# Turning kv by VectorE blocks and a DRAM round trip instead of TensorE, in a gated cross-attention block with routed experts

## The reference, cut to what matters

```
xn = layernorm(ctx; gamma_m, beta_m);  ln = layernorm(layernorm(x); gamma_l, beta_l)
q = ln @ Wq + bq;   kv = concat(xn, ln) @ Wkv + bkv          # per batch row: 128 keys
out = softmax(q k^T / sqrt(128)) v                            # 8 heads
x = x + tanh(g_xattn) * (out @ Wo + bo)
p = softmax(layernorm(x) @ Wr + br);  two largest of 8 experts
x = x + tanh(g_ffn) * sum_e p_e * (relu(xn @ W1_e + b1_e) @ W2_e + b2_e)
```

## Time and profile before

| what | value |
|---|---|
| time, median of 3 runs (lowest to highest) | 797.5 us (796.06 to 798.2) |
| span of the profiled execution, first to last instruction | 795.7 us; a run's time is 1.8 us longer at the median |
| PE busy | 760.7 us, 96% |
| PEld, DVE, ACT, POOL busy | 81%, 66%, 62%, 56% |
| chain that ended last | PE 77%, issue 6%, POOL 6%, DVE 5%, ACT 4% |
| granted TensorE clock, mean | 0.993 |
| DMA | 119.42 MB, mean 150 GB/s |

### The profile page before, as it was taken

One profiled execution on the slowest core, in us unless ns is written; L12 is line 12 of the kernel. 1 busy time (PEld: TensorE's weight loads), 2 busy tenths in 40 slices (PEclk: granted clock), 3 DMA queues, 4 the chain that ended last, 5 costly groups with the idle time before them and its releaser, 6 DMA issues.

```text
span 795.7 us, 17460 instructions
## 1 busy us (share of the span) xinstructions
PE 760.7 (96%) x5392; PEld 643.6 (81%) x5392; DVE 528.3 (66%) x1829; ACT 496.9 (62%) x1630; POOL 446.1 (56%) x455
## 2 busy tenths in 40 slices
PE   7999999999999999999999999999999999979788
PEld 6778777777888988778988878898877888868765
DVE  5636677685857567677658776776868567565536
ACT  3677777676766566766656667565567665554522
POOL 2233264646552544785655586665568566556664
PEclk9999999999999999999999999999999999999999
DMA  7735151542454642174754226664414555634523
GB/s 198 209 150 194 60 213 69 211 146 81 145 188 154 205 153 72 38 231 143 237 189 143 65 76 218 206 212 163 127 54 140 180 191 188 212 112 116 154 77 87
DMA packets 119791, 119.42 MB, mean 150 GB/s; under 512 B 14585, under 2 KB 94994, under 8 KB 119698
## 3 DMA queue, kind: packets, MB, share of 16 engines
q1 hardware_dynamic: 111088, 102.41, 39.1%
q0 software_dynamic: 7680, 15.74, 6.8%
q10 hardware_dynamic: 930, 0.15, 0.1%
HBM read 35.94 MB, written 41.55 MB: 97 GB/s over the span
## 4 chain that ended last, share of the span: by engine, by line
PE 77%; issue 6%; POOL 6%; DVE 5%; ACT 4%; DMA 1%; another core or an unknown queue 1%; SPq 1%; POOLq 0%; ACTq 0%; DVEq 0%
PE shared L1426 13%; PE batch L1364 11%; PE batch L1377 11%; PE hid_ps L1294 8%; PE xy_ps L1308 7%; PE batch L1372 6%; PE shared L1217 3%; PE shared L1219 3%; PE shared L1218 3%; ACT probs L746 3%; PE batch L1308 2%; POOL probs L676 2%; PE xy_ps L1271 2%; POOL yg L666 2%; PE batch L1354 2%
## 5 line engine op out<-in xcount | busy, mean ns | idle before, releaser
L676 POOL TENSOR_TENSOR probs<-probs,rsums 128x512 f32<-128x512 f32 x128 | 132.9, 1039 | 231.7 <-DVE rsums L1147 230.1
L746 ACT ACTIVATE probs<-batch,neg_max 128x128 f32<-128x128 f32 x512 | 180.5, 374 | 2.0 <-DVE neg_max L1151 2.0
L651 POOL DMA_INDIRECT sorted_x<-xn,row_of x120 | 124.4, 1036 | 33.6 <-issue 28.7
L827 ACT ACTIVATE qT<-shared,tb 128x512 f32<-128x512 f32 x128 | 87.2, 696 | 85.6 <-PE shared L1219 72.4
L1377 PE MATMUL batch<-pT_sb,kvn 128*128 128x512 f32 x256 | 133.7, 604 | 2.9 <-ACT pT_sb L754 2.9
L1364 PE MATMUL batch<-kvT,qT 128*128 128x128 f32 x1024 | 135.4, 275 | 0.8 <-ACT qT L827 0.8
L1426 PE MATMUL shared<-M,oT 128*128 128x128 f32 x1024 | 125.5, 276 | 0.3
L1364 PEld LDWEIGHTS batch<-kvT,qT 128*128 128x128 f32 x1024 | 124.4, 192 | 1.2 <-ACT qT L827 1.2
L1426 PEld LDWEIGHTS shared<-M,oT 128*128 128x128 f32 x1024 | 119.4, 192 | 1.6 <-issue 1.6
L746 ACT ACTIVATION_READ_ACCUMULATOR probs<-batch,neg_max 128x1 f32 x512 | 110.2, 215 | 0.0
L1147 DVE RECIPROCAL rsums<-sums 128x4 f32<-128x4 f32 x128 | 22.7, 178 | 130.4 <-ACT probs L746 119.9
(11 more groups left out here) (168 smaller groups left out, 1243.4 us busy)
## 6 DMA issues: line engine op xcount, KB each, us to landing
wt<-wall SPq DMA_DIRECT2D x124, 321.0 KB
sorted_x<-yg SPq DMA_DIRECT2D x36, 512.0 KB, 4.8
xt<-sorted_x SPq DMA_DIRECT2D x162, 64.0 KB
sorted_y<-y_sb SPq DMA_DIRECT2D x78, 128.0 KB
kv<-in_ctx_dram SPq DMA_DIRECT2D x16, 256.0 KB
kv<-in_x_dram SPq DMA_DIRECT2D x16, 256.0 KB
xres<-in_x_dram SPq DMA_DIRECT2D x32, 128.0 KB
out_dram<-x SPq DMA_DIRECT2D x15, 256.0 KB
```

Source lines behind the costliest of these rows:

```text
L651: nc.gpsimd.indirect_dma_start(xs[k % SETS][:, :], bass.IndirectOffsetOnAxis(ap=row_of[:, g, choice, c:c + 1], axis=0), xn[:, g % 2, c, :] ...
L676: nc.gpsimd.tensor_tensor(pv, pv, rsums[:, m % 2, :].unsqueeze(2).broadcast_to([P, 4, P]), ALU.mult).then_inc(probs_ready, 1)
L746: last = nc.scalar.activation(probs[:, m % 2, c * P:(c + 1) * P], batch_ps[m % BANKS][:, c * P:(c + 1) * P], ACT.Exp, bias=neg_max[:, m % ...
L827: nc.scalar.activation(qT[:, g % 2, :, number, :], sh[:, :].rearrange("p (b i) -> p b i", b=GB), ACT.Identity, bias=tb[:, number:number + ...
```

## The change

From the second group on, kv is no longer turned on TensorE. VectorE turns it in 32x32 blocks into `kv_blocks`, half a group (four rows) at a time, right behind the shift of that half (slots 7 and 0). SP stores the blocks to a DRAM scratch array (slots 0 and 1) and, when the store has landed, loads them back with the blocks permuted into kvT (slots 1 and 2). `kv_blocks` is one buffer, so the second half's turn waits for the landing of the first half's store. kvT is laid out by blocks of 32 keys. `split_latents` moves to slot 3 and waits for both loads; so do the first scores of a group. The queries move to slots 4 to 7, two in each, at places "c", "c", "c" and "b". The first group keeps TensorE's turn, with four copies in place of each one. kvn grows from 18 to 20 rows so that the four rows of a half are adjacent, and two small tiles (`filled`, `past`) now lie in existing ones.

```diff
-KVN = 18
+KVN = 20
 ...
-    3: [("query", 1, 0, "a"), ("query", 1, 1, "b")],
-    4: [("project", 0, 0, "a"), ("turn_x", -1, 0, "b"), ("query", 1, 2, "c")],
-    5: [("router", -1, 0, "a"), ("query", 1, 3, "b"), ("query", 1, 4, "c")],
-    6: [("project", 0, 1, "a"), ("query", 1, 5, "b")],
-    7: [("query", 1, 6, "a"), ("query", 1, 7, "b")],
+    4: [("project", 0, 0, "a"), ("turn_x", -1, 0, "b"), ("query", 1, 0, "c"), ("query", 1, 1, "c")],
+    5: [("router", -1, 0, "a"), ("query", 1, 2, "c"), ("query", 1, 3, "c")],
+    6: [("project", 0, 1, "a"), ("query", 1, 4, "c"), ("query", 1, 5, "c")],
+    7: [("query", 1, 6, "b"), ("query", 1, 7, "b")],
 ...
+ and (what != "turn_kv" or g == 0)
 ...
-        kvT = sb("kvT", [P, 2, GB, P])
+        kvT = sb("kvT", [P, 2, BLOCKS, GB, BLOCK])
+        kv_blocks = sb("kv_blocks", [P, BLOCKS, 4, BLOCK])
 ...
+            def keep_blocks(g, half):
+                sp.wait_ge(blocks_turned, 2 * (g - 1) + half + 1)
+                wait(sp, got_kvT[half], 16 * (g - 1))
+                sp.dma_start(kv_turning[half], kv_blocks[:, :, :, :].rearrange("p b i j -> p (b i j)")).then_inc(blocks_kept[half], 16)
+            def load_turned(g, half):
+                sp.wait_ge(blocks_kept[half], 16 * g)
+                wait(sp, scores_ready, GB * (g - 1))
+                sp.dma_start(kvT[:, g % 2, :, 4 * half:4 * half + 4, :].rearrange("p a i j -> p a (i j)"),
+                             kv_turning[half].rearrange("(a m) (b x) -> (m b) a x", a=BLOCKS, b=BLOCKS)).then_inc(got_kvT[half], 16)
             for n in range(FIRST, LAST + 1):
                 weights(n)
                 s = n % GB
+                for half in range(2):
+                    g = n // GB + 1
+                    if s == half and 0 < g < G:
+                        keep_blocks(g, half)
+                    if s == half + 1 and 0 < g < G:
+                        load_turned(g, half)
 ...
+            def turn_blocks(n):
+                for half in range(2):
+                    g = (n - NORMALISE[2 * half + 1]) // GB
+                    if (n - NORMALISE[2 * half + 1]) % GB == 0 and 0 < g < G:
+                        dve.wait_ge(kv_ready, 4 * g + 2 * half + 2)
+                        if 2 * g + half > 2:
+                            dve.wait_ge(blocks_kept[1 - half], 16 * (g - 1 + half))
+                        first = (GB * g + 4 * half) % KVN
+                        nc.vector.transpose(kv_blocks[:, :, :, :].rearrange("p b i j -> p i b j"),
+                                            kvn[:, first:first + 4, :].rearrange("p i (m b) -> p i b m", b=BLOCKS)).then_inc(blocks_turned, 1)
             def split_latents(n, s):
-                if s == 2 and 0 <= g < G:
+                if s == (2 if g == 0 else 3) and 0 <= g < G:
+                    for half in range(2):
+                        wait(dve, got_kvT[half], 16 * g)
 ...
                 normalise_kv(n)
+                turn_blocks(n)
 ...
             def scores(m):
+                    for half in range(2):
+                        wait(pe, got_kvT[half], 16 * g)
-                                            kvT[:, g % 2, b, :], start=True, stop=True)
+                                            kvT[:, g % 2, :, b, :], start=True, stop=True)
```

More of the change, by code:

```diff
@@ L171 @@
     2: [("project", -1, 3, "a"), ("table", -2, 0, "c")],
[5 rows of a table removed]
-}
[4 rows of a table added]
+}
+BLOCK = 32
+BLOCKS = P // BLOCK
 def plan_shared():
@@ L186, in plan_shared @@
             g = n // GB + off
-            if 0 <= g < (SORTED if what == "place" else G) and (what != "table" or g in LAST_GROUP):
+            if 0 <= g < (SORTED if what == "place" else G) and (what != "table" or g in LAST_GROUP) and (what != "turn_kv" or g == 0):
                 bank = at % 2
@@ L285, in flamingo @@
         tile_id = sb("tile_id", [P, 1])
-        filled = sb("filled", [P, E, J])
+        filled = eq[:, :, :, :].rearrange("p c e f -> p (c e f)")[:, 0:E * J].rearrange("p (e j) -> p e j", e=E)
         n_tiles = sb("n_tiles", [P, E])
@@ L295, in flamingo @@
         table = sb("table", [2, NCH, P], I32)
-        past = sb("past", [P, max(CHUNKS) * 8, E - 1])
+        past = gt[:, :, :, :].rearrange("p c e f -> p (c e f)")[:, 0:max(CHUNKS) * 8 * (E - 1)].rearrange("p (m e) -> p m e", e=E - 1)
         skip = sb("skip", [P, max(CHUNKS) * 8])
@@ L361, in flamingo @@
         xs = [nc.dram_tensor(f"sorted_x{p}", (E * ROWS, D), F32).ap() for p in range(SETS)]
+        kv_turning = [nc.dram_tensor(f"kv_turning{half}", (P, BLOCKS * 4 * BLOCK), F32).ap() for half in range(2)]
         ys = [nc.dram_tensor(f"sorted_y{p}", (max(TILES) * TILE, D), F32).ap() for p in range(SETS)]
@@ L391, in flamingo @@
         kv_ready = sem("kv_ready")
+        blocks_turned = sem("blocks_turned")
+        blocks_kept = [sem("blocks_kept0"), sem("blocks_kept1")]
+        got_kvT = [sem("got_kvT0"), sem("got_kvT1")]
         scores_ready = sem("scores_ready")
@@ L821, in read_out @@
                 if what == "turn_kv":
-                    wait(act, scores_ready, GB * (g - 1))
-                    nc.scalar.activation(kvT[:, g % 2, 4 * number:4 * number + 4, :].rearrange("p b j -> p (b j)"),
-                                         sh[:, :], ACT.Copy).then_inc(shared_out[bank], 1)
+                    for b in range(4):
+                        last = nc.scalar.activation(kvT[:, g % 2, :, 4 * number + b, :], sh[:, b * P:(b + 1) * P].rearrange("p (a j) -> p a j", a=BLOCKS),
+                                                    ACT.Copy)
+                    last.then_inc(shared_out[bank], 1)
                 elif what == "query":
@@ L918, in normalise_kv @@
                     shift_kv((n - NORMALISE[k]) // GB, k)
+            def turn_blocks(n):
[8 more added lines that the diff above has]
+                                            kvn[:, first:first + 4, :].rearrange("p i (m b) -> p i b m", b=BLOCKS)).then_inc(blocks_turned, 1)
             def split_latents(n, s):
                 g = n // GB + 1
-                if s == 2 and 0 <= g < G:
+                if s == (2 if g == 0 else 3) and 0 <= g < G:
                     wait_shared(dve, shared_out, "turn_kv", g, 1)
+                    for half in range(2):
+                        wait(dve, got_kvT[half], 16 * g)
                     wait_shared(dve, shared_full, "query", g - 1, 7)
-                    nc.vector.tensor_copy(latT_hi[:, :, :], kvT[:, g % 2, :, L:P]).then_inc(latT_done, 1)
+                    mine = kvT[:, g % 2, L // BLOCK:BLOCKS, :, :].rearrange("p a b j -> p b a j")
+                    nc.vector.tensor_copy(latT_hi[:, :, :].rearrange("p b (a j) -> p b a j", j=BLOCK), mine).then_inc(latT_done, 1)
                     dve.wait_ge(latT_done, 2 * g + 1)
-                    nc.vector.tensor_tensor(latT_lo[:, :, :], kvT[:, g % 2, :, L:P], latT_hi[:, :, :].bitcast(F32),
-                                            ALU.subtract).then_inc(latT_done, 1)
+                    nc.vector.tensor_tensor(latT_lo[:, :, :].rearrange("p b (a j) -> p b a j", j=BLOCK), mine,
+                                            latT_hi[:, :, :].rearrange("p b (a j) -> p b a j", j=BLOCK).bitcast(F32), ALU.subtract).then_inc(latT_done, 1)
             def measure_rows(n, s):
```

## The result

The kernel after takes 840.62 us (median of 4 runs, 839.67 to 842.93) where the kernel before takes 797.16 in the same comparison: ratio 1.0553, 95% interval 1.0538 to 1.0567. It is slower, as forecast, but by 43.5 us where 19.7 were forecast, and outside the range of 797 to 834. A ratio with its interval is of fast runs alone, and one of e14's twelve runs, at 4334.61 us, is left out of it.

A forecast was written before the change was run, and what follows sets the result against it. Prediction: TensorE bounds slots with expert tiles, ScalarE's 3.7 us ring several slots without. Terms -5.3 - 4.2 - 3.2 - 4.0 + 9.7 + 0.7 + 19.2 + 4.8 + 2.0 = +19.7 gave 817 us, range 797 to 834.

The forecast's parts named there:

- Store, load and waits: Term for kv's round trip through DRAM and SP's queue: taken as 0, up to +20 us over 15 groups.
- the cover: Time to spare before transfers delay anyone: 0.7 us for the second half's turn, 1.5 us for its store and load.
- two copies issued in 1.14 us fit, barely: Slot 50's weight fetch on SP's queue would wait for the turn until about 253.4; its tile starts near 258.
- or SP is held by its store of the tile before: Part of the rival that kvT lands late, VectorE standing in slot 3: 837 to 847 us, chance 12%.
- I take 0.70: Time of one VectorE block turn, from the median 0.67 us of its 128x512 float32 rows; bounds 0.42 and 1.50.
- if the block turns take over 1 us: One of the signs that would show the prediction wrong: VectorE's block turns taking over 1 us.
- its own rule: VectorE's turns delay slots 0 and 1 without tiles: two turns less 0.32 and 0.13 us of gaps; term +4.8 us.
- TensorE's turn -5.3: Turn_kv leaving TensorE saves 0.88 us in each of six slots 1 with a tile, 0 in the nine without.
- The places: Queries moved: slot 3 gives -4.2, -3.2, -4.0; slots 4 to 6 with tiles +9.7, +0.7; groups without tiles +19.2 us.
- the ring of 3.7: ScalarE's chain from pT_sb through product, oT and exponentials to the next pT_sb, 3.7 us per slot whatever PE does.
- The +2.4 in slots 4 to 7: Loss per group without tiles from query work and late place "c" readouts holding ScalarE; 2.4 x 8 = +19.2 us.
- The prologue's +2.0: Start of the kernel: 8 small copies for 2, queries no longer filling gaps, first group's wait; +2.0 us, range 0 to 3.

The follow-up runs named there:

- e14: Kernel before with only groups 7, 10 and 13 turned by VectorE, their queries in the new slots, round trip right behind the fetch; ratio 0.9996.
- e1: Kernel before with only the queries' new slots and places, kv still turned on TensorE; 816.38 us.
- e3: Kernel after with the round trip moved behind the weight fetch, the tile's store and its row load on SP's queue; 833.23 us.
- e10: Kernel after with SP's order changed to weight fetch, then round trip, then the tile's store and rows; 834.73 us.
- e11: Kernel after with stores and loads cut to 16 of 128 partitions from group 2 on, the load no longer permuting; 836.08 us.
- e13: Kernel after with the changes of e10 and e11 together; 829.01 us.
- e8: Kernel before with only groups 7, 8, 10, 11, 13, 14 turned by VectorE, round trip last in SP's order, queries as before; ratio 1.0314.
- e5: Kernel before with TensorE's turn of kv and its copies left out from the third group on, nothing in their place; 792.82 us.
- e7: e1 plus VectorE's two block turns a group into a buffer nobody reads, no store or load, TensorE still turning; 829.13 us.
- e4: Kernel after with VectorE's block transpose replaced by a plain copy between the same access patterns; 839.5 us.

## Why the prediction was wrong

The step that failed: "Store, load and waits ... I take 0 for all of it; if the cover is gone, up to 1.3 us in each of 15 groups, +20." The cover was gone. Slots 2 and 3 are 14.9 us longer than with the places alone, and TensorE waits 14.3 us for weights there, where in e1 it waits for none: by e3, e10, e11 and e13 because the weights leave late behind the round trip on SP's queue, and because of the transfers themselves. The prediction had seen the place ("two copies issued in 1.14 us fit, barely"), looked at one fetch, slot 50's, and took a margin near zero for zero. Slot 50 itself waits 0.73 us, and slots 51, 67, 75 and 91 wait 1.05, 3.42, 1.31 and 2.25. That TensorE's clock would fall behind such a wait, as in slot 67 (5.21 us busy, 3.79 in e1), stands in no term. Its rival "or SP is held by its store of the tile before" had the time right (837 to 847, measured 840.6), but by luck: it told of VectorE standing for kvT, which in the kernel after is 0.6 us once; the hybrid e8 shows that rival for real.

The second failure is a size. "I take 0.70" for a block turn: measured 1.11 us, by the prediction's own words a sign of being wrong ("if the block turns take over 1 us"). With its own rule (two turns and their wait less 0.45 us of gaps) the groups 2 to 5 would pay 1.87, measured 1.73; groups 8, 11 and 14, put at nothing, pay 0.6 each, group 0, not counted, pays 1.31, and group 1, put at 0.6, pays 1.36. The term is 11.5, not 4.8. The reading that the Trainium skill, "VectorE: DVE Perf Modes", § The three transpose paths, allowed (an estimate of 1.24 us from its 311 ns for a 128x128 bf16 tile) was nearer than the median of VectorE's other 128x512 rows. That is in part luck, as the turn with neighbouring numbers took 0.71.

The steps that held: TensorE's turn -5.3, measured alone -5.2 (e5), though the kernel after keeps 4.1 of it: in slots 73 and 97 TensorE stands 0.28 and 0.30 us for pT_sb, with VectorE busy 4.40 of 4.73 us in slot 73. The places: -4.2 - 3.2 - 4.0 + 9.7 + 0.7 + 19.2 = +18.2, measured +19.2 in the slots (e1). Slot 3 gave 10.8 of 11.4 there, but in other parts, so that its sum is partly luck. Groups 7, 10 and 13 gave 1.77 each, not 0.5: their slots 3 fall to 2.79 us, so the ring of 3.7 is no floor for a slot that follows a tile. Groups 0 to 3 gave nothing in e1, and groups 5, 8, 11 and 14 1.1 of 3.2. The +2.4 in slots 4 to 7 of a group without tiles is 2.28, and its reason holds: 1.4 of work and 1.0 of late readouts were forecast, 1.20 of work and 1.08 of waiting are read. The prologue's +2.0 was wrong, it is 1.1 us shorter. One sum does not come out: with turns at 1.5 us and places at 3.5 the forecast's own bounds reach 834 (817 + 8.2 + 8.8), not 830.

In sum, of 42.8 us of span: places +19.2, VectorE's turns +11.5, TensorE's turn -5.2, slots 2 and 3 +14.9, the rest of slots 0 and 1 +1.6 (1.1 of it in slots 73 and 97), slot 4 +1.2, prologue and tail -0.3 (42.9 by these rounded sums). What lengthens slot 4 stays open.

## What to carry to other kernels

Before a wait is put into an in-order DMA queue, list each transfer behind it with its own slack; a margin near zero on one of them is a cost on the others. Work taken from the busiest engine is worth only the slots in which that engine ends last: leave it out altogether first (e5), and if that bound is small, no clever replacement pays. Moving work to a full engine can cost its whole duration where a short chain (here reciprocals, multiply, turn of the probabilities) stands behind it in that engine's order: 1.14 us for a turn of 1.11 in slot 1, 0.59 in slot 0 (e7). And before time lost on TensorE is called waiting, look at its busy time and granted clock in the same slot, as in e4 and e8.

## What the runs showed of the hardware

VectorE's turn of 128x512 float32 in 32x32 blocks takes 1.11 us with its input in steps of 16 bytes, 0.71 with neighbouring numbers; a plain copy with the same steps takes 0.63. A permuting load of 256 KB in runs of 512 bytes took 4.0 us in e8 from issue to VectorE's start (260.65 to 264.63), with weights before and behind it on the same queue. The Trainium skill, "VectorE: DVE Perf Modes", § The three transpose paths, warns that a plain DMA copy which transposes by its access pattern is 19 times slower than the DMA's own transpose when the innermost destination stride is large; the innermost runs of this load are contiguous, as its blocks are turned before, and it shows nothing of the kind.

A wait of TensorE can be paid for again in its clock. After it had stood 3.42 us in slot 67 of the kernel after, it worked at half clock from 378.86 to 382.27 and was busy 5.21 us in that slot, 3.79 in e1. In the six slots 3 of e8 that makes 13.5 us beside 19.1 of idle time.
